# Layer 1's outer products read both factors from SBUF; the copy of the unshifted fields to PSUM goes

## The reference

```python
def _cin(x0, conv_params, split_flags):
    B, _, D = x0.shape
    x = x0
    results = []
    for (W, b), split in zip(conv_params, split_flags):
        h = x.shape[1]
        z = jnp.einsum('bhd,bmd->bhmd', x, x0).reshape(B, h * x0.shape[1], D)
        xk = jax.nn.relu(jnp.einsum('oc,bcd->bod', W, z) + b[None, :, None])
        if split:
            half = xk.shape[1] // 2
            x, xk = (xk[:, :half], xk[:, half:])
        else:
            x = xk
        results.append(xk)
    return jnp.sum(jnp.concatenate(results, axis=1), axis=2)

pooled = _cin(sparse_embed, [(W1, b1), (W2, b2), (W3, b3)], [True, True, False])
return pooled @ Wo.T + bo
```

## Time and profile before

| what | value |
|---|---|
| median of three runs | 475.0 us |
| the profiled execution's own time | 474.85 us |
| its span (first to last instruction on the core) | 472.9 us |
| PE busy | 443.7 us, 94% |
| DVE busy | 430.4 us, 91% |
| POOL busy | 407.2 us, 86% |
| ACT busy | 318.4 us, 67% |
| mean granted TensorE clock | 0.996 of full |

### The profile page before, as it was taken

One profiled execution on the slowest core, in us unless ns is written; L12 is line 12 of the kernel. 1 busy time (PEld: TensorE's weight loads), 2 busy tenths in 40 slices (PEclk: granted clock), 3 DMA queues, 4 the chain that ended last, 5 costly groups with the idle time before them and its releaser, 6 DMA issues.

```text
span 472.9 us, 5975 instructions
## 1 busy us (share of the span) xinstructions
PE 443.7 (94%) x1600; PEld 299.8 (63%) x1600; DVE 430.4 (91%) x490; ACT 318.4 (67%) x397; POOL 407.2 (86%) x147
## 2 busy tenths in 40 slices
PE   0796999899999999999999999999999999999997
PEld 0243556466767767676767766676766767677774
DVE  1499996988999999999999999999999999999997
ACT  1456785576868777585868767685877768577761
POOL 0145698589999999999999999999999999999995
PEclk9998999999999999999999999999999999999999
DMA  8999829999995959779495969969495962922010
GB/s 215 251 253 213 178 53 223 223 206 217 200 225 114 233 116 225 155 170 229 102 228 114 222 133 206 194 138 228 115 229 119 227 143 66 201 44 46 21 23 1
DMA packets 22608, 76.84 MB, mean 162 GB/s; under 512 B 5827, under 2 KB 5827, under 8 KB 18116
## 3 DMA queue, kind: packets, MB, share of 16 engines
q1 hardware_dynamic: 22596, 76.70, 74.0%
HBM read 61.48 MB, written 0.00 MB: 130 GB/s over the span
## 4 chain that ended last, share of the span: by engine, by line
PE 76%; DMA 9%; DVE 4%; SPq 4%; POOL 3%; issue 2%; ACT 2%; DVEq 0%; POOLq 0%
PE y_ps L784 24%; PE y_ps L790 14%; PE y_ps L772 14%; PE y_ps L774 14%; PE y_ps L780 6%; DMA shifted<-xt_dram 6%; PE y_ps L796 3%; POOL zl L553 3%; DVE z L602 2%; DMA a_rep<-x_sb 2%; DMA b_fac<-xt_dram 1%; SPq L335 1%; SPq L319 1%; SPq L344 1%; SPq L321 1%
## 5 line engine op out<-in xcount | busy, mean ns | idle before, releaser
L553 POOL TENSOR_TENSOR zl<-z,zh 128x1024 fp32r<-128x1024 f32 (+1 forms) x141 | 405.2, 2908 | 48.9 <-ACT zh L470 48.7
L602 DVE TENSOR_TENSOR z<-a_ps,b_fac 128x512 f32<-128x512 f32 (+2 forms) x256 | 272.3, 1086 | 25.5 <-PE y_ps L796 11.9
L470 ACT ACTIVATE zh<-z 128x1024 fp32r<-128x1024 f32 (+1 forms) x141 | 176.3, 1251 | 118.4 <-DVE z L602 117.9
L790 PE MATMUL y_ps<-zl,w_high 128*128 128x512 f32 x330 | 152.2, 554 | 6.2 <-POOL zl L553 6.2
L772 PE MATMUL y_ps<-zh,w_high 128*128 128x512 f32 x330 | 130.8, 396 | 4.7 <-ACT zh L470 3.8
L774 PE MATMUL y_ps<-zh,w_low 128*128 128x512 f32 x330 | 129.1, 391 | 0.0
L784 PE MATMUL y_ps<-z,w_raw 128*128 128x512 f32 x252 | 128.4, 591 | 0.0
L790 PEld LDWEIGHTS y_ps<-zl,w_high 128*128 128x128 f32 x330 | 61.5, 188 | 75.6 <-issue 58.7
L772 PEld LDWEIGHTS y_ps<-zh,w_high 128*128 128x128 f32 x330 | 61.9, 188 | 21.4 <-issue 3.6
L774 PEld LDWEIGHTS y_ps<-zh,w_low 128*128 128x128 f32 x330 | 62.1, 188 | 13.4
L784 PEld LDWEIGHTS y_ps<-z,w_raw 128*128 128x128 f32 x252 | 47.3, 188 | 10.4
(11 more groups left out here) (42 smaller groups left out, 176.9 us busy)
## 6 DMA issues: line engine op xcount, KB each, us to landing
b_fac<-xt_dram SPq DMA_DIRECT2D x52, 512.0 KB, 8.7
shifted<-xt_dram SPq DMA_DIRECT2D x64, 256.0 KB, 4.9
a_rep<-x_sb SPq DMA_DIRECT2D x87, 128.0 KB, 2.4
shifted<-xt_dram SPq DMA_DIRECT2D x64, 128.0 KB, 5.1
b_fac<-xt_dram SPq DMA_DIRECT2D x24, 256.0 KB, 9.4
a_rep<-x_sb SPq DMA_DIRECT2D x58, 64.0 KB, 2.1
w_raw<-w_dram SPq DMA_DIRECT2D x2, 640.0 KB, 13.6
w_raw<-w_dram SPq DMA_DIRECT2D x2, 384.0 KB, 17.3
```

The costliest lines, as they stand in the source:

```text
L470: nc.scalar.activation(zh[:, slot, 0:end - native, :], z[:, slot, native:end, :], ACT.Copy).then_inc(zh_ready, 1)
L553: nc.gpsimd.tensor_tensor(zl[:, slot, 0:end - native, :], z[:, slot, native:end, :], zh[:, slot, 0:end - native, :].bitcast(F32), ALU.subtract
L602: return nc.vector.tensor_tensor(dst, factor.unsqueeze(1).to_broadcast(list(dst.shape)), others, ALU.mult)
L790: mm = nc.tensor.matmul(y, wh[layer][:, w, :], zl[:, slot, t, :], start=False, stop=end_here)
```

## The change

The bank `x_ps`, the semaphore `x_in_psum` and the helper `x_to_psum` with its four calls on ScalarE are removed. The factor of layer 1's products is, for every chunk, the sixth slot of `shifted` in SBUF, which was until now the source of the copy. VectorE waits for the load (`x_loaded`), as it did, and no longer for the copy. The multiplications, their order and their outputs are the same.

```diff
-        x_ps = psum("x_ps", [P, CH])
...
-        x_in_psum = sem("x_in_psum")
...
-            def x_to_psum(c):
-                act.wait_ge(x_loaded, c * (16 * X_DMAS))
-
-                nc.scalar.activation(x_ps[:], shifted[:, bass.ds((c % XSLOTS) * (XT * CH) + XREP * CH, CH)], ACT.Copy
-                                     ).then_inc(x_in_psum, 1)
-
...
-                            x_to_psum(1)
...
-                            x_to_psum(2)
...
-                            x_to_psum(3)
...
-                    if pos == 5 and exists(i + 1):
-                        x_to_psum(i + 1)
...
                 if layer == 1:
                     others = shifted[:, bass.ds((c % XSLOTS) * (XT * CH), XT * CH)
                                      ].rearrange("p (t n) -> p t n", t=XT)
+                    factor = others[:, XREP, :]
                     if is_native(q):
-                        factor = others[:, XREP, :]
                         dve.wait_ge(x0_loaded, 16 * X_DMAS)
                     else:
-                        factor = x_ps[:]
-                        dve.wait_ge(x_in_psum, c)
                         dve.wait_ge(x_loaded, c * (16 * X_DMAS))
```

## The result

The changed kernel takes 543.3 us (541.79 to 543.58, 4 runs) where the kernel before took 474.82 us in the same comparison: ratio 1.1438, 95% interval 1.1414 to 1.1461. The profiled execution took 543.14 us, its span is 541.2 us: 68.3 us more than the span before. An execution more than 1.5% above the fastest of the same kernel is left out of every ratio here; that happened once, in e6.

A forecast was written before the change was run, and what follows sets the result against it. TensorE sets the pace, with VectorE and GpSimd within 4%. Added to 474.85 us: 3.4 (chunk 2) + 3.4 (chunk 3) - 1.4 (copy wait) + 75 (chunks 4 to 15) = 555.3, said as 555; range 496 to 565.

The forecast's parts named there:

- the period: Time from one layer 1 product A to the next in later iterations: 33.2 us against 26.94, +6.25 each.
- chunk 4: First of chunks 4 to 15, each charged the full 6.25 us, 75 us for the twelve.
- the ramp: Early chunks: chunk 1 costs 0, chunk 2 +3.4 us, chunk 3 +3.4 us less 1.4 for the copy.
- Standing still, whole instructions: Layer 1's A, B, C with two SBUF inputs and GpSimd's subtractions exclude each other for a whole instruction.
- Rival 3: No standing still for layer 1's products; only the 1.4 us wait and copies count: 473.5 us; chance 0.03.
- Who goes first: When one engine's instruction ends and both have the next ready, they take turns, older request first: 555 us; chance 0.58.
- Rival 1: VectorE keeps its turn through A, B and C, standing still once: +1.6 us an iteration, 499 us; chance 0.20.
- rival 2: GpSimd keeps its turn while it has work; A waits for positions 7 and 8: +3.9, 525 us; chance 0.15.
- VectorE's lead over TensorE: Hides a part once: TensorE is 3.4 us late in the first such iteration, then takes 6.25 in each later one.
- The -1.4 us for the copy: VectorE's single wait for a copy, in the ramp at chunk 3, goes with the copies: -1.4 us.
- TensorE's idle time: Sign in the changed profile: TensorE idle some 6 us an iteration, waiting for VectorE at position 0.
- The copies at nothing, the same price alone: Fifteen ScalarE copies, 8.9 us, cost nothing; A takes 1218 ns from PSUM, 1222 ns from SBUF when GpSimd is idle.

The follow-up runs named there:

- e6: Kernel before, copies kept, only C (third of layer 1's products) reading its factor from SBUF: median 500.05 us of the three lower executions, ratio 1.0529.
- e1: Kernel before with all 15 copies to PSUM still made, but layer 1's products reading the factor from SBUF: 541.61 us, ratio 1.1408.
- e2: Kernel before with only chunk 1's copy to PSUM; later chunks multiply with that stale factor from PSUM: 474.77 us, ratio 1.0000.
- e7: Changed kernel; at positions 7, 8 and 0 GpSimd subtracts one column and sets the rest by memset: 473.33 us, ratio 0.9971.
- e8: Changed kernel; at positions 7, 8 and 0 GpSimd subtracts one column and copies z to zl for the rest: 481.08 us, ratio 1.0132.
- e12: Kernel before (factor in PSUM, copies made) with GpSimd memsets for all but one column at positions 7, 8 and 0: 473.37 us, ratio 0.9970.
- e3: Changed kernel with layer 1's products in the order B, A, C: 519.35 us, ratio 1.0939.
- e11: Changed kernel; at positions 7, 8 and 0 GpSimd subtracts one tile (128x512) an instruction: 519.55 us, ratio 1.0952.
- e9: Kernel before with chunk 3's copy to PSUM made at position 1 of iteration 2 in place of position 4: 474.77 us, ratio 1.0001.

## Why the prediction was right, and where a term was off

The forecast was 555 us, measured 543.3: direction and mechanism right, the loss 80 us forecast against 68 measured. The 12 us between them are 5.8 of the period, 4.0 of chunk 4 and 2.2 of the ramp.

*Standing still, whole instructions.* Right. The indicators were A, B, C at about 2.4, 4.1, 3.6 us, each ending 0.6 to 1.1 us behind a subtraction; measured 2.10, 3.98, 3.42 and 1.09, 0.56, 1.10. The trace of before held a third split behind a subtraction, which the prediction doesn't show: 34.11 to 37.70, again 0.82 us behind GpSimd's end (33.42 + 3.46). With 512, 768 and 1024 elements the distance is 0.56, 0.82 and 1.09 us, each 0.13 under the undisturbed duration (0.69, 0.95, 1.22): it grows as the instruction's own work does. e1 and e2 place the loss in the operand, e7, e8 and e12 in GpSimd's reading. Rival 3, no exclusion, is dead by A's 2.10 us, and by e7 beside e8. In the words of the Trainium skill, "SBUF — State Buffer", Who interferes with whom, the conflict is with a GpSimd instruction "that reads SBUF, not with one that only writes it"; e7's overlap and e8's standstill agree. The note under Mode Summary of the Trainium skill's "Advanced Engine Details and Errata" speaks of two-port instructions alone and would have had no place for it. The prediction read more into that section than it holds: it is Instruction Support there that gives a product of two tensors no two-port mode, and GPSIMD Details on the same page names two SBUF inputs as a conflict too, so the two pages don't contradict each other as the prediction has it.

*Who goes first.* Turns, as forecast, in all even iterations of the changed kernel, where B took 3.96 to 3.98 us each time. Rival 1 (VectorE runs through) fails by that B, rival 2 (GpSimd keeps its turn) by A going ahead of position 8. But turns are not a rule: of 11 even iterations, GpSimd kept its turn in 3 in e6, and in one each in e1 (A, 5.54 us), e3 (B took 4.92 us where the others took 1.4 to 1.7) and e11 (A, 5.73 us). The prediction took the older request to be served first, and cites the Trainium skill for issue order; in e6 at 195.87 C's request (193.08) was the older one, position 0's input being rounded only at 193.66, and GpSimd went first. What decides it stays open. That it never happened in the changed kernel's trace is in part luck of that execution: e1, with the same products, had it once.

*The period, 33.2 forecast, 32.6 measured.* The term was mis-sized by taking start-to-start distances for the time that one engine holds the other. An instruction that stands still seems to have its start-up behind it when its turn comes, the 0.13 us above. From the end of position 7 (301.69) to position 1's product (309.92) it is 8.23 us; I had 1.14 + 3.46 + 0.60 + 2.36 + 1.19 = 8.75. GpSimd's own stretches show what a product holds: 4.50 - 3.54 = 0.96 for A and 2.84 - 2.42 = 0.42 for B against the earlier trace rows, not 1.14 and 0.60. The rest of the period was right: 24.38 us from position 1's product to the next end of position 7, 24.44 forecast. Over the ten even periods (chunk 5's A at 137.59 to chunk 15's at 463.52, 32.59 each) this is 5.8 us of the 12 missed.

*Chunk 4.* I charged a full 6.25; it cost 2.2 (chunk 4's A came 3.2 us late, chunk 5's 5.4). Chunk 4's group in the changed kernel:

```profile
107.19 2.10 DVE L589 TENSOR_TENSOR z<-shifted 128x1024 f32 x1 [0.19 <-issue]
109.21 0.69 DVE L589 TENSOR_TENSOR zx_ps<-shifted 128x512 f32 x1
109.81 4.48 DVE L589 TENSOR_TENSOR z<-shifted 128x1024 f32 x1
```

and GpSimd beside it, position 8:

```profile
109.36 3.85 POOL L540 TENSOR_TENSOR zl<-z,zh 128x1536 fp32r<-128x1536 f32 x1 [1.16 <-ACT zh L462]
```

GpSimd still waited for ScalarE when A was done, so B (109.21) came ahead of position 8, and C stood behind position 8 (end 113.21) alone. The group loses one turn fewer than the later ones: behind it VectorE is 4.1 us later than before it. And 1.9 of these were made up by chunk 5's A, because the kernel before had waited for TensorE in this iteration, and the changed one, being late, had not:

```profile
111.02 2.36 DVE L602 TENSOR_TENSOR z<-a_ps,b_fac 128x1536 f32<-128x1536 f32 x2 [0.46 <-PE y_ps L790]
...
114.46 1.23 DVE L602 TENSOR_TENSOR z<-a_ps,b_fac 128x1024 f32<-128x1024 f32 x1 [0.48 <-PE y_ps L796]
...
117.38 2.36 DVE L602 TENSOR_TENSOR z<-a_ps,b_fac 128x1536 f32<-128x1536 f32 x2 [0.50 <-PE y_ps L796]
```

That is VectorE's lead over TensorE, which hides a part once, as forecast; I had it used up at chunk 3. Together the two are 4.0 us of the 12.

*The ramp.* I forecast 5.4 us of lateness from chunks 2 and 3. Against before, chunk 3's A started 1.2 us late (73.95 for 72.79) and chunk 4's 3.2 (107.19 for 104.01). Chunk 2 went as forecast: A took 4.43 us, the products behind it came 2.65 us late (62.97 for 60.32), and 1.4 of that went where the kernel before had waited for the copy. Chunk 3's group stood as long as a later one (2.24, 3.97 and 3.41 us), 6.5 us in all where I had charged 3.4. But its loss wasn't passed on in full, since the kernel before waited there for loads, 1.41 and 1.85 us, as this row of before shows beside the one above:

```profile
82.03 2.35 DVE L602 TENSOR_TENSOR z<-a_ps,b_fac 128x1536 f32<-128x1536 f32 x2 [1.85 <-DMA b_fac<-xt_dram]
```

The late products found their loads landed. These two waits, 3.3 us, are what the ramp's term lacked; that chunk 3's group was charged 3.1 too little nearly cancels them, and that is luck. Smaller waits of before took 1.0 us more by chunk 4's A (the product of 86.26 for 82.03 is 4.2 late). The -1.4 us for the copy is less clear. e9 shows it at nothing, but in the kernel before, where the load's wait takes its place. In e1, where the copies are made and VectorE doesn't wait for them, ScalarE is late as well, and chunk 3's copy ends at 75.75, 1.4 us behind the start of A (74.34):

```profile
75.17 0.58 ACT L402 ACTIVATE x_ps<-shifted 128x512 f32<-128x512 f32 x1
```

So a changed kernel that still waited for the copy would have started that A later by about that much; it was not run. Together the ramp gave 2.2 us of the 12. Chunk 15's own group cost 6.2, as forecast.

*TensorE's idle time.* The sign was some 6 us an iteration at position 0. It was 4.2, and only 1.78 and 0.48 of it there, behind VectorE; the rest was spent waiting for GpSimd's remainders, at position 8 (0.66) and later (1.04), and for another subtraction of VectorE's (0.25).

*The copies at nothing, the same price alone.* Right: e2 at ratio 1.0000, e1 with all copies no slower than the changed kernel, and C at 1.21 us in e3 with both operands in SBUF.

## What to carry to other kernels

When VectorE and GpSimd work side by side, count VectorE's SBUF inputs: the second one made it stand still behind GpSimd instructions that read SBUF (a subtraction and a copy here), and GpSimd behind it, for whole instructions, however small its own is. A copy of one factor to PSUM by an engine with time to spare (here 0.6 us an iteration) buys that off; if it can't be had, arrange the instructions so that GpSimd has nothing ready when they come, or make GpSimd's shorter; each bought back 24 of the 68 us here. A stretched duration in a profile can be waiting; compare its end with the end of the other engine's instruction. And before a wait in a ramp is given a price, look at what the instruction behind it waits for.

## What the runs showed of the hardware beyond that

- A GpSimd memset of 1.37 us overlapped a VectorE product with two SBUF inputs fully, a GpSimd copy of 1.92 us not at all (e7, e8).
- With both engines' next instruction ready, VectorE was not always served after GpSimd's: 3 of 11 times in e6 it stood through a second subtraction (6.2 to 6.3 us in place of 3.9), and once in e11 through four in a row (5.73 us in place of 1.6).
- A VectorE product that had stood still ended 0.56 us (512 elements) or 1.09 us (1024) behind GpSimd's end, in every kernel here.
- The length of one idle stretch doesn't tell if the granted TensorE clock falls: in e11 it fell to its 1.2 GHz level behind 1.85 us of idling (295.11) and stayed at full behind 1.84 us (142.53). With the fall an iteration of e11 took 30.7 us, and 29.04 to 29.5 without. The changed kernel's stayed at 1.00 from 100 to 460 us with idle stretches of up to 1.78 us.
